# Eight experts on every token, or two experts on tokens sorted by expert

## The reference, cut to what matters

```python
xn = layernorm(x)
out = x + attn(xn, 4 layers) + ffn(xn)

def block(h, p):                              # one layer of attn
    m = retention(h, Wkqv) @ Wm1 + bm1
    a, gate = split(m, 2)
    m = groupnorm1(a * silu(gate) @ Wm2 + bm2)
    y = m + h
    return layernorm(gelu(y @ Wf1 + bf1) @ Wf2 + bf2 + y)

def ffn(inputs):                              # once, on xn
    logits = einsum('bsd,ed->bse', inputs, Wg)          # 8 experts
    topw, sel = top_k(logits, 2)
    cw = sum(one_hot(sel) * softmax(topw))              # weight of each expert, 0 for six of eight
    y = einsum('bsd,eod->bseo', inputs, We) + be        # each expert is a 128x128 matrix
    return einsum('bseo,bse->bso', y, cw)
```

## Time and profile before

| | value |
|---|---|
| time, median of 3 runs | 446.3 us (446.29 to 446.39) |
| the profiled execution's own time | 446.27 us |
| its span (first to last instruction) | 444.5 us |
| PE, PEld busy | 423.9 us (95%), 325.7 us (73%) |
| DVE busy | 391.7 us (88%) |
| ACT busy | 262.8 us (59%) |
| POOL busy | 242.4 us (55%) |
| granted TensorE clock, mean | 0.992 of full speed |
| HBM read, written | 5.60 MB, 2.10 MB |

### The profile page before, as it was taken

One profiled execution on the slowest core, in us unless ns is written; L12 is line 12 of the kernel. 1 busy time (PEld: TensorE's weight loads), 2 busy tenths in 40 slices (PEclk: granted clock), 3 DMA queues, 4 the chain that ended last, 5 costly groups with the idle time before them and its releaser, 6 DMA issues.

```text
span 444.5 us, 8154 instructions
## 1 busy us (share of the span) xinstructions
PE 423.9 (95%) x2356; PEld 325.7 (73%) x2356; DVE 391.7 (88%) x1218; ACT 262.8 (59%) x541; POOL 242.4 (55%) x287
## 2 busy tenths in 40 slices
PE   8999889999999999999999999999999999998781
PEld 8888767777777777778777777777777777775440
DVE  5878989899988989888988899988988899899957
ACT  2957366655656565665755655665566565555551
POOL 3695214446564666456644455444444446567895
PEclk9999999999999999999999999999999999999996
DMA  7800000000000000000000000000000000000102
GB/s 239 268 1 1 0 2 1 1 2 1 1 1 1 0 3 0 1 1 1 2 1 1 0 2 0 1 1 1 0 2 0 1 2 1 4 22 24 48 25 71
DMA packets 13499, 8.22 MB, mean 18 GB/s; under 512 B 608, under 2 KB 13456, under 8 KB 13456
## 3 DMA queue, kind: packets, MB, share of 16 engines
q1 hardware_dynamic: 13376, 7.68, 5.6%
q10 hardware_dynamic: 80, 0.02, 0.0%
HBM read 5.60 MB, written 2.10 MB: 17 GB/s over the span
## 4 chain that ended last, share of the span: by engine, by line
PE 84%; DVE 9%; issue 2%; ACT 2%; DMA 1%; POOL 1%; DVEq 0%; ACTq 0%; POOLq 0%
PE bank L264 6%; PE pair L361 6%; PE bank L268 6%; PE bank L265 6%; PE pair L367 6%; PE bank L471 6%; PE bank L272 6%; PE bank L343 6%; PE bank L434 6%; PE bank L467 5%; PE bank L351 5%; PE pair L369 5%; PE pair L396 3%; PE pair L264 3%; PE pair L265 3%; PE pair L268 3%
## 5 line engine op out<-in xcount | busy, mean ns | idle before, releaser
L1302 POOL TENSOR_TENSOR y_part<-y,y_part 128x512 fp32r<-128x512 f32 x32 | 40.7, 1273 | 109.4 <-ACT y_part L736 109.4
L729 ACT ACTIVATE hg<-vt,gn_c,g_prev 128x512 f32<-128x512 f32 x32 | 26.1, 815 | 55.4 <-DVE gn_c L1081 55.4
L718 ACT ACTIVATE tanh_g<-bank,params 128x512 f32<-128x512 f32 x32 | 22.0, 687 | 46.4 <-PE bank L268 46.4
L367 PEld LDWEIGHTS pair<-va,scores 128*128 128x128 f32 x256 | 38.5, 191 | 14.3 <-issue 14.0
L769 ACT ACTIVATE va<-bank,ln_off,ln_r 128x128 f32<-128x128 f32 x128 | 48.2, 457 | 1.1
L1318 POOL TENSOR_TENSOR sum_four<-prod 128x512 f32<-128x512 f32 x32 | 41.1, 1283 | 7.7 <-issue 7.3
L1276 POOL TENSOR_TENSOR gn_r<-gn_v,minus_half 128x1 f32<-128x1 f32 x32 | 18.7, 584 | 48.5 <-DVE gn_v L1068 48.5
L367 PE MATMUL pair<-va,scores 128*128 128x129 f32 x256 | 44.4, 275 | 0.7 <-ACT kqv_t L684 0.7
L1281 POOL TENSOR_TENSOR ln_r<-ln_v,minus_half 128x4 f32<-128x4 f32 x32 | 32.7, 1023 | 15.6 <-ACT ln_v L761 15.6
L264 PE MATMUL bank<-ot,b_w 128*128 128x512 f32 x64 | 40.6, 635 | 0.0
L1023 DVE TENSOR_TENSOR ot<-pair,ot 128x512 fp32r<-128x512 f32 x32 | 22.1, 691 | 17.8 <-ACT ot L701 17.8
(11 more groups left out here) (177 smaller groups left out, 1224.1 us busy)
## 6 DMA issues: line engine op xcount, KB each, us to landing
x_in<-in_L_attn_x_dram SPq DMA_DIRECT2D x8, 256.0 KB, 4.8
out_dram<-x_in SPq DMA_DIRECT2D x8, 256.0 KB, 2.3
wf<-in_L_attn_Wf_dram SPq DMA_DIRECT2D x2, 512.0 KB, 6.1
kqv<-in_L_attn_Wkqv_dram SPq DMA_DIRECT2D x1, 576.0 KB, 5.5
gelu<-in_L_ffn_We_dram SPq DMA_DIRECT2D x1, 512.0 KB, 6.7
wm<-in_L_attn_Wm_dram SPq DMA_DIRECT2D x1, 384.0 KB, 5.8
wm<-in_L_attn_Wm_dram SPq DMA_DIRECT2D x1, 256.0 KB, 4.5
zt<-in_L_ffn_be_dram SPq DMA_DIRECT2D x16, 4.0 KB
```

The lines of the kernel that those rows point to most:

```text
L367: mm = pe.matmul(dst, scores[:, n % 2, of], va[:, n % NB, c, 0:D + 1], start=True, stop=(c == 0))
L1302: pool.tensor_tensor(y_part[:, 1, :], y[:, n % 2, :], y_part[:, 0, :].bitcast(F32), ALU.subtract).then_inc(y_rest, 1)
```

## The change

The experts no longer run on all tokens. Each token's normalised row is written twice to a buffer in HBM, once in the region of each of its two experts; every expert's region is rounded up to whole tiles of 128 rows, so 72 tiles (32 + 32 + 8) always suffice. The steps:

- DVE and PE work out the row number of every token for both of its experts (`count_chosen`, `place_rows`) and the expert of every tile (`number_tiles`, `place_tiles`).
- SP fills the buffer with zeros in 9 DMAs of 512 KB, and stores the eight turned expert matrices to HBM.
- POOL scatters: for each of 32 chunks two indirect DMAs of 128 rows of 512 bytes (`scatter`), four chunks per slot over POOL's slots 38 to 45.
- The 72 tiles run in 18 groups of four (`GROUP`). SP loads the rows of a group with one DMA and the four weight matrices with four, each of an address that it reads from SBUF (`value_load`). PE turns the four tiles, ACT copies them, PE multiplies them (in f32), ACT copies the results and SP stores them. Two groups per slot, in PE's slots 14 to 23; two buffers of each kind. Both products of a group use PSUM bank 7.
- POOL gathers: for each chunk two indirect DMAs (`gather`), three chunks per slot over POOL's slots 59 to 70, with four buffers.
- DVE adds the two gathered rows of every token, each times its share, to x (`combine`), three chunks per slot from its slot 28 on.

`scale_last` and `add_result` are on DVE for all 8 sequences (`ON_POOL = 0`). The layer-0 input has a tile of its own (`va0`), since the scatter reads it later. The order of all engines' lists is a new one: `project(n - 1)` and `score(n - 1)` now stand in the same slot, `turn_o(n - 1)` at its end, `feed_a` one slot later than before, and several PSUM banks changed. POOL's slot numbers run 33 ahead of DVE's for the same item. The sums on POOL, the weighing on DVE and the splitting of xn and of the expert weights are gone.

```diff
+    TILES = 2 * CHUNKS + E
+    GROUP = 4
+    GROUPS = TILES // GROUP
+    PICKED = 4
+    ON_POOL = 0
...
+            def load_group(g):
+                if g >= 2:
+                    sp.wait_ge(tiles_done, g - 1)
+                arrived = group_in[g % 2]
+                rows_in_group = sorted_rows[g * GROUP * P:(g + 1) * GROUP * P, :]
+                sp.dma_start(sorted_x[:, g % 2, :, :], rows_in_group.rearrange("(j p) d -> p j d", p=P)).then_inc(arrived, 16)
+                for j in range(GROUP):
+                    t = g * GROUP + j
+                    e = sp.value_load(expert_of[0:1, t:t + 1], min_val=0, max_val=E - 1)
+                    sp.dma_start(tile_w[:, g % 2, j, :], expert_rows_t[bass.ds(e, 1), :, :].rearrange("e d o -> d (e o)")).then_inc(arrived, 16)
+
+            sp.wait_ge(tile_step, TILED)
+            sp.wait_ge(expert_out, 16)
+            sp.wait_ge(scattered, 16 * 2 * CHUNKS)
+            load_group(0)
+            load_group(1)
+            for g in range(GROUPS):
+                rows_in_group = sorted_results[g * GROUP * P:(g + 1) * GROUP * P, :]
+                sp.wait_ge(results_set, g + 1)
+                sp.dma_start(rows_in_group.rearrange("(j p) d -> p j d", p=P), result[:, g % 2, :, :]).then_inc(group_out[g % 2], 16)
+                if g + 2 < GROUPS:
+                    load_group(g + 2)
...
+            def turn_tiles(n):
+                g = n
+                pe.wait_ge(group_in[g % 2], 16 * (GROUP + 1) * (g // 2 + 1))
...
+                turn(TILE_IN_BANK, lambda j: sorted_x[:, g % 2, j, :]).then_inc(tiles_turned, 1)
+
+            def ask_tiles(n):
+                g = n
+                pe.wait_ge(tiles_set, g + 1)
...
+                for j in range(GROUP):
+                    mm = pe.matmul(TILE_OUT_BANK[:, j * D:(j + 1) * D], sorted_t[:, g % 2, j * P:(j + 1) * P], tile_w[:, g % 2, j, :],
+                                   start=True, stop=True)
...
+                step(turn_tiles, 2 * (n - 15) + 1, 0, GROUPS)
...
+                step(ask_tiles, 2 * (n - 15) + 1, 0, GROUPS)
...
+                if n == 5:
+                    pe.wait_ge(place_step, 20)
+                    fold(1, banks[5])
...
+                step(turn_tiles, 2 * (n - 14), 0, GROUPS)
...
+                step(ask_tiles, 2 * (n - 14), 0, GROUPS)
...
-            def weigh(n, h, bank, done, weighed):
...
+            def combine(n):
                 k, c = divmod(n, C)
...
+                dve.wait_ge(picked_in[i], 32 * (n // PICKED + 1))
                 dve.wait_ge(bias_set, k + 1)
...
+                dve.scalar_tensor_tensor(x_in[:, k, c, :], picked[:, i, 0, :], total[:, 1, n:n + 1], x_in[:, k, c, :],
+                                         ALU.mult, ALU.add).then_inc(half_added, 1)
+                dve.wait_ge(half_added, n + 1)
+                dve.scalar_tensor_tensor(x_in[:, k, c, :], picked[:, i, 1, :], second_share[:, n:n + 1], x_in[:, k, c, :],
+                                         ALU.mult, ALU.add).then_inc(x_added, 1)
...
+            def scatter(n):
+                k, c = divmod(n, C)
...
+                for j in range(2):
+                    pool.indirect_dma_start(sorted_rows[:, :], bass.IndirectOffsetOnAxis(ap=rows_of[:, j, n:n + 1], axis=0),
+                                            va0[:, k, c, 0:D], None).then_inc(scattered, 16)
+
+            def gather(n):
+                if n == 0:
+                    for h in range(2):
+                        pool.wait_ge(group_out[h], 16 * ((GROUPS + 1 - h) // 2))
+                read(pool, n, x_added, PICKED)
+                for j in range(2):
+                    pool.indirect_dma_start(picked[:, n % PICKED, j, :], None, sorted_results[:, :],
+                                            bass.IndirectOffsetOnAxis(ap=rows_of[:, j, n:n + 1], axis=0)).then_inc(picked_in[n % PICKED], 16)
...
+                step(norm_factor, n - 39)
...
+                step(rest_of_y, n - 37)
+                step(scatter, 4 * (n - 38))
+                step(gather, 3 * (n - 60) + 2)
+                step(group_factor, n - 36)
...
+                step(scatter, 4 * (n - 38) + 1)
+                step(gather, 3 * (n - 59))
+                step(gather, 3 * (n - 59) + 1)
+                step(scatter, 4 * (n - 38) + 2)
+                step(scatter, 4 * (n - 38) + 3)
```

More of the change, by code:

```diff
@@ new lines, in slot @@
+                step(feed_b, n - 5)
+                if n == 9:
+                    pe.wait_ge(ot_rest, 8)
+                    keep_busy(2, banks[0])
+                if n == 8:
+                    pe.wait_ge(expert_set, 2)
+                    turn_route(0, banks[7])
+                if n == 5:
+                    pe.wait_ge(logits_set, 4)
+                    turn_experts(1, banks[7])
+                step(turn_z, n - 6)
+                if n == -10:
+                    turn_in(2, banks[3])
@@ new lines, in slot @@
+                if n == -24:
+                    turn_params(banks[1])
+                step(mix_out, n - 3)
+                if n == -29:
+                    keep_busy(5, banks[0])
+                if n == -25:
+                    turn_in(1, banks[5])
+                if n == -30:
+                    fold(0, banks[6])
+                step(mix_a, n - 2)
+                step(project, n - 1)
+                step(ask_tiles, 2 * (n - 15) + 1, 0, GROUPS)
+                if n == -23:
+                    pe.wait_ge(xt_set, 1)
+                    ask_gate(0, banks[2])
@@ new lines, in slot @@
+                if n == -34:
+                    turn_kqv(0, banks[3])
+                if n == 1:
+                    pe.wait_ge(b_set, 1)
+                    turn_in(4, banks[6])
+                if n == 2:
+                    pe.wait_ge(logits_set, 1)
+                    ask_gate(4, banks[2])
+                step(score, n - 1)
+                if n == 10:
+                    pe.wait_ge(kqv_t_set, 3)
+                    fold(2, banks[7])
+                if (n - 8) % 4 == 0:
+                    step(route_bias, n - 8)
@@ L621, in slot @@
[L621 to L633 removed]
+                    turn_in(5, banks[3])
@@ new lines, in slot @@
+                step(back_b, n - 5)
+                if n == 3:
+                    pe.wait_ge(kqv_shifted, 2)
+                    turn_in(7, banks[5])
+                if n == 2:
+                    ask_gate(5, banks[2])
+                step(ask_tiles, 2 * (n - 14), 0, GROUPS)
+                step(back_a, n - 5)
+                step(gram, n)
+                if n == 6:
+                    pe.wait_ge(b_set, 2)
+                    shift_weights(3, banks[5])
+                if n == -4:
+                    ask_gate(1, banks[2])
@@ L634, in _ @@
+                if n == 3:
+                    pe.wait_ge(xt_set, 7)
+                    ask_gate(6, banks[7])
+                if n == 4:
+                    pe.wait_ge(logits_set, 3)
+                    turn_kqv(1, banks[2])
+                step(turn_o, n - 1)
+            for n in range(-40, 38):
                 slot(n)
@@ L875, in _ @@
+                if n == -11:
+                    normalise_in(3)
+                step(round_y, n - 3)
+                step(set_vt, n - 7, 0, 24)
+            for n in range(-77, 38):
                 slot(n)
@@ L1086, in set_y @@
                 read(dve, n, y_rest, 2)
+                read(dve, n, z_set, 2)
                 dve.wait_ge(gn_scale, n + 1)
@@ L1235, in slot @@
-                step(divide_second, n - 1)
-                step(weigh_a, n - 5)
-                if n == 1:
-                    read_in(7)
-            for n in range(-35, 42):
+                if n == 0:
+                    read_in(6)
+                step(norm_aggr, n - 6)
+                if n == -2:
+                    read_in(4)
+                if (n - 9) % 4 == 0:
+                    step(add_biases, n - 9)
+                if n == 8:
+                    rest_of_route(0, banks[7])
@@ new lines, in slot @@
+                step(add_result, n - 8, 24)
+                if n == 5:
+                    place_rows(banks[5])
+                step(group_stats, n - 3)
+                step(past_third, n - 1)
+                if n == -50:
+                    read_in(0)
+                step(group_aggr, n - 3)
+                step(combine, 3 * (n - 28) + 1)
+                if n == 13:
+                    rest_of_b(2, banks[7])
+                if n == 3:
+                    shift_kqv(2, banks[5])
+                step(group_means, n - 3)
@@ L1241, in _ @@
+            for n in range(-50, 40):
                 slot(n)
@@ L1418, in _ @@
+                if n == -10:
+                    in_factor(3)
+            for n in range(-42, 71):
                 slot(n)
```

921 lines of the change are left out of this document (412 added, 509 removed).

## The result

The changed kernel takes 483.7 us (median of 4 runs, 481.6 to 486.3) against 446.3: a ratio of 1.084, with an interval of 1.078 to 1.090. It is 37.4 us slower. The forecast was 440, faster; the time lies inside the range, on its wrong side.

What follows compares the result with a forecast made beforehand. PE was taken to bound the middle at 12.38 us per item. The terms summed as 444.5 - 37.8 + 23.9 + 1 - 1.5 + 4 + 3 + 1 + 0 = 438.1, plus 1.8 outside the span: about 440 us, range 428 to 495.

Steps and rivals of the forecast that it cites:

- the first: Whole kernel: PE sets the pace from 78.2 to 387.4 us (the middle), 12.38 us per item; in the tail, DVE and POOL.
- dense experts out: PE's 27 full slots: six passes of 512 columns fewer per slot, 1.40 us each slot, -37.8 us.
- new order, idle products moved: PE's start: fourteen matmuls that only keep PE busy leave, -1.5 us; no term for the new order.
- tile products and their loads: PE's slots 14 to 23: 18 groups of 1.33 us, +23.9; SP's loads making PE wait, +3 (0 to +15).
- counting and placing: Counting the chosen and numbering tiles, +1 us; DVE's placing chains, which PE's fold(1) and mix_gate await, +4 (0 to 9.6).
- indirect DMAs: POOL's queue: eight per scatter slot make it 11.1 against 11.0 us, +1; gather slots of 9.1 stay under 11.0.
- combining: DVE from slot 28: three combines add 1.9 to 2.6 us per slot; 0 to +2.5 us over four slots, taken as 0.
- PE's terms: PE's project starts 11.0 us apart before slot 14 and 13.7 apart while tiles run, with no idle time on PE.
- c: The time one indirect DMA holds POOL: taken as 1.0 us, between 0.49 and 2.5.
- the first rival: POOL becomes the bound if c is over about 1.07: 457 us at 1.2, 490 at 1.5; chance 0.38.
- The sign that I named: PE waiting for y_part or ACT for ln_mr, released by POOL between two indirect DMAs, would show c over 1.07.
- The tail: From the last project to the end: 57.1 us before, 57 after; taken as 0, at best -4.

Runs made afterwards that it cites:

- both_by_sp: The changed kernel with the 64 scattering and 64 gathering indirect DMAs replaced by plain DMAs of the same size on SyncE's queue; 472.1 us.
- tiles_alone: The changed kernel's order with the 18 tile groups, their loads, copies and stores, but no counting, placing, scatter, gather or combining; 449.9 us.
- order_alone: The changed kernel's order with all expert work left out (counting, placing, scatter, tile products, gather, combining); 427.2 us.
- before_no_experts: The kernel before without the expert products, their weighing, sums and additions and the rounding of x for them; 411.0 us.

## Why the prediction was wrong

The step that failed is the first: that an edit "counts in the middle if it takes or adds PE work, or lifts another engine past PE", and beside the middle only in the tail. The stage in which the pipeline fills is in neither. From it came a sum with one term for each operation and none for the new order, which rewrote the lists of the engines; the runs showed 16.2 us in its place. Two more terms were taken at nearly nothing, the indirect DMAs (11.7) and the combining (13.0). The forecast's terms beside what the runs gave:

```
term                                    forecast    measured
dense experts out                         -37.8       -36.7   (447.7 - 411.0)
new order, idle products moved             -1.5       +16.2   (427.2 - 411.0)
tile products and their loads       +23.9, +3         +22.7   (449.9 - 427.2)
counting and placing                  +1, +4           +8.0   (483.7 - 475.7)
indirect DMAs                              +1         +11.7   (483.7 - 472.1)
combining                                   0         +13.0   (2 x 6.5; 12.9 by windows)
sum                                        -6.4       +34.9   (37.4 in the whole kernel)
```

Of the 41.3 us between the two sums 17.7 are the order, 13.0 the combining, 10.7 the indirect DMAs and 3.0 the placing; the dense experts add 1.1 and the tiles take 4.2 off. The second half of the combining was not run by itself; the two windows of both_by_sp and of tiles_alone, 108.8 against 95.9 us, give 12.9 for both halves.

- *PE's terms* were right: plain slots of 11.0, tile slots of 13.5, no idle time of PE among the tiles. Only the 11.0 ahead of slot 14, which I had named as a sign, isn't there: those slots take 9.8 to 17.6. The same view that gave them, a full PE from 78.2 us on the earlier trace rows, says nothing about a stage in which PE isn't full for a reason of order.
- *The order*: 16.2 us, the largest miss. It could have been asked of the diff: in the new lists `project` of an item stands behind `turn_o` and `mix_a` of the one ahead. I noted only that `score` follows `project` in one slot, and took it as a gain for the tail. The products that only keep PE busy, which I took out at 1.5, didn't leave: in order_alone they stand in the chain at 11.05 for 1.56 us, ahead of `project(0)`. Once PE is full the order costs nothing here (155.7 us from `project(13)` to `project(27)` in order_alone, 157.1 in before_no_experts); in the first thirteen items it does, I take it because there is too little other work.
- *SyncE's loads*: +3 was not paid. The 64 KB of a tile's weights land after 1.8 us and the rows after 3.1 in the median, and PE waits for nothing at 187 to 365 us.
- *Placing*: it costs 8.0 us, near the upper bound of 9.6 instead of the value 4. The reason I gave, PE's own work ahead of the wait, holds in part for the rows: PE waits 3.0 of a chain of 8.0. It doesn't hold for the tiles: PE waits 3.0 of a chain of 3.0.
- *GpSimd*: c is 1.26, with the 0.30 between two that I hadn't split off, over the threshold of 1.07. So the condition of the first rival came true, and its formula gives the slots (3.1 + 8 x 1.26 = 13.2; 13.7 and 13.4 measured). But its price did not: 11.7 us instead of some 24 (8 x 2.2 and 4 x 1.6), I take it since the slots it stretches were long by the order already. The sign that I named, ACT waiting for `ln_mr`, is there in the tail (9.6 us, beside the gather) but not beside the scatter (0.2). Without any indirect DMA the kernel is still 5.7% slower than before: that rival isn't the cause of the loss, though it ends on the right side. The rule of the Trainium skill that I weighed ("DMA: Bandwidth & Descriptors", section "SWDGE vs HWDGE vs iDMA", GpSimd locked out of writing descriptors beside VectorE) shows little here: the 64 scatters take 0.954 at least, 0.958 in the median and 1.54 at most, with DVE busy 76% of that stage.
- *Combining*: DVE has 11.6 of 12.0 us in each of the four slots, the upper end of my 10.9 to 11.6, and the slot is 12.0, over it, I take it because the two additions of a chunk follow each other and leave gaps (DVE waits only 0.3 us for other engines in the four slots). I took the lower end with the argument that L1134's median came from slots with POOL's sums. That argument held for the single operation (0.34 and 0.35 in the median) but not for the sum, whose base I had at 9.0 and which tiles_alone shows at 9.3.
- *The tail*: 66.3 against 57. Its parts are combining and the gather on GpSimd; the lower clock has up to 5.0 in it, by the estimate above.
- Right in size and worth nothing: without POOL's sums `mixed` on DVE takes 0.69 in the median, not 1.11, which gives DVE 13 us back in 32 items. In the middle PE sets the pace, so they bring nothing there.

No kernel of these beats the one before with its output whole. The parts say why: the sorted experts cost 56.5 us in this order, the dense ones 36.7. In the old order, if the parts add up there too, they would come to some 467.

## What to carry to other kernels

Price a reordering as a term of its own, above all where the pipeline fills: ask for each engine what now stands ahead of the first instruction of the next item, and whether that waits for another engine. A stage in which one engine is full tells nothing of the stages in which none is. And before the costs of a change are worked out, run in thought the kernel in its new order with its new products and all other new costs at nothing: here (427 + 23) that alone was above the time before.

## What the runs showed of the hardware

A DMA with a list of 128 rows of 512 bytes holds GpSimd for 0.96 us and the next follows 0.30 later, for scatter and gather alike; 64 such cost some 81 us of its queue. In a slot with eight of them that is 10.1 us beside 3.1 of arithmetic.

One addition of a `combine` takes 0.34 or 0.35 us alone and up to 1.48 beside a GpSimd operation with two operands in SBUF. The changed kernel's timeline of DVE, then that of POOL:

```profile
391.24 0.34 DVE L1240 SCALAR_TENSOR_TENSOR x_in<-picked,total,x_in 128x128 f32<-128x128 f32 x1
391.62 1.48 DVE L1243 SCALAR_TENSOR_TENSOR x_in<-picked,second_share,x_in 128x128 f32<-128x128 f32 x1
```

```profile
391.66 1.29 POOL L1415 TENSOR_TENSOR y_part<-y,y_part 128x512 fp32r<-128x512 f32 x1 [0.51 <-ACT y_part L811]
```

Both begin within 0.04 us and end within 0.15 us of each other. Of the 64 additions seven take over 0.5 us, each beside an L1415, and all seven end 0.14 or 0.15 us after it, wherever they began (their lengths are 1.19 to 1.48). The Trainium skill, "SBUF — State Buffer", section "SBUF: two separate sides", has this as a lock on a shared port pair, held for a whole instruction, of a VectorE operation with two SBUF inputs against a GpSimd operation that reads SBUF. The rows agree: the end of the GpSimd operation sets DVE's end, so DVE waits for it rather than running slower. Which of the two held the lock first they don't show, since this DVE operation is recorded as beginning 0.04 us before the other.
